# One relative-table turn a step earlier, and two row sums a few turns earlier, in a relative-position attention stage

## The reference

```
logits = einsum('bhqd,bhkd->bhqk', q, k) + einsum('bhqd,qkd->bhqk', q, rk)
w = softmax(logits)
out = einsum('bhqk,bhkd->bhqd', w, v) + einsum('bhqk,qkd->bhqd', w, rv)
x = x + out @ Wo.T + bo
```

## Time and profile before

| what | value |
|---|---|
| median of three executions | 4339.19 us |
| profiled execution | 4342.39 us, span 4340.7 us |
| PE (matmul) busy over the span | 3962.5 us, 91% |
| DVE busy | 3486.0 us, 80% |
| ACT busy | 2981.4 us, 69% |
| POOL busy | 1446.1 us, 33% |
| mean granted TensorE clock | 0.951 |

### The profile page before, as it was taken

The page is one execution under the profiler, slowest core; times in us unless marked ns, Lnnn a source line. Parts: engine busy times, 40 slices in busy tenths (PEclk is TensorE's granted clock), DMA queues, the critical chain, the costliest instruction groups (busy, mean ns, idle before and its releaser), DMA issues. The chain is left out here.

```text
span 4340.7 us, 77253 instructions
## 1 busy us (share of the span) xinstructions
PE 3962.5 (91%) x26592; PEld 2108.1 (49%) x26592; DVE 3486.0 (80%) x6304; ACT 2981.4 (69%) x5821; POOL 1446.1 (33%) x1405
## 2 busy tenths in 40 slices
PE   8699999999999999996799999999999996599997
PEld 5355555555455555544433333333333333499997
DVE  6788888888888888835688898888888872477775
ACT  4078888888788878881148888888888883266664
POOL 0356666666666666641100000000000001522232
PEclk9599999999999999998879999999999997699998
DMA  8566666666676667635652323223323303676664
GB/s 312 152 160 171 165 171 165 170 165 170 159 172 165 170 160 172 164 81 188 201 99 31 53 38 47 44 40 46 50 36 48 43 7 89 172 218 172 170 179 110
DMA packets 486195, 556.39 MB, mean 128 GB/s; under 512 B 60260, under 2 KB 426836, under 8 KB 476524
## 3 DMA queue, kind: packets, MB, share of 16 engines
q1 hardware_dynamic: 465980, 526.94, 49.1%
q0 software_dynamic: 19824, 24.52, 3.4%
HBM read 347.67 MB, written 206.76 MB: 128 GB/s over the span
## 5 line engine op out<-in xcount | busy, mean ns | idle before, releaser
L371 DVE TENSOR_REDUCE pa_pm<-pa_psA 128x2 f32<-128x1024 f32 x1024 | 1207.9, 1219 | 134.9 <-PE pa_psA L460 134.8
L1098 ACT ACTIVATE ra_p<-ra_psS 128x512 f32<-128x512 f32 x2048 | 1082.0, 606 | 315.1 <-PE ra_psS L1175 223.8
L434 ACT ACTIVATE pa_p<-pa_psS 128x512 f32<-128x512 f32 x2048 | 1063.5, 604 | 247.4 <-PE pa_psS L486 243.1
L1009 DVE TENSOR_REDUCE ra_pm<-ra_psA 128x1 f32<-128x896 f32 x1024 | 1112.7, 1087 | 147.6 <-PE ra_psA L1133 132.7
L486 PE MATMUL pa_psS<-pa_qs,pa_zs 50*128 50x512 f32 x2048 | 793.2, 464 | 77.6 <-ACT pa_p L434 64.2
L460 PE MATMUL pa_psA<-pa_zs,pa_qs 48*128 48x512 f32 x2048 | 796.7, 472 | 38.0 <-DMA pa_zs<-k_halves 17.8
L1133 PE MATMUL ra_psA<-ra_zs,ra_qs 48*128 48x512 f32 x2048 | 729.9, 450 | 19.1 <-DVE ra_pm L1011 8.4
L1175 PE MATMUL ra_psS<-ra_qs,ra_zs 50*128 50x512 f32 (+3 forms) x2176 | 699.6, 406 | 28.4 <-ACT ra_p L1098 17.9
L486 PEld LDWEIGHTS pa_psS<-pa_qs,pa_zs 50*128 50x128 f32 x2048 | 342.2, 185 | 626.0 <-ACT pa_p L434 607.0
L1206 PE MATMUL ra_psO<-ra_p,ra_vs 128*32 128x512 f32 (+3 forms) x6400 | 551.0, 449 | 0.0
L1175 PEld LDWEIGHTS ra_psS<-ra_qs,ra_zs 50*128 50x128 f32 x2176 | 350.4, 186 | 409.0 <-ACT ra_p L1098 318.4
(11 more groups left out here) (247 smaller groups left out, 4947.2 us busy)
## 6 DMA issues: line engine op xcount, KB each, us to landing
relative_rows<-ra_rst SPq DMA_DIRECT2D x128, 512.0 KB, 3.9
ra_blk<-window_rows SPq DMA_DIRECT2D x128, 512.0 KB
mo_w_raw<-ffn_W SPq DMA_DIRECT2D x58, 1024.0 KB, 5.4
ra_zs<-k_halves SPq DMA_DIRECT2D x192, 248.0 KB, 7.1
ra_dl<-relative_rows SPq DMA_DIRECT2D x128, 256.0 KB, 4.7
window_rows<-ra_pc SPq DMA_DIRECT2D x128, 256.0 KB
pa_qs<-q_halves SPq DMA_DIRECT2D x192, 128.0 KB, 6.2
pa_zs<-k_halves SPq DMA_DIRECT2D x192, 128.0 KB, 6.8
```

Source lines behind the costliest of these rows:

```text
L371: dve.reduce_max(pm[:, par, 2 * a:2 * a + 2], psA[w][:, :, :], AX.X).then_inc(s_am.h, 1)
L434: act.activation(pr[:, i % NPR, :], psS[:, slot(i), :], ACT.Exp).then_inc(s_ex.h, 1)
L1009: dve.reduce_max(pm[:, q, i, 2 * left:2 * left + 1], psA[w][:, lo:lo + 2 * G - P], AX.X).then_inc(s_far.h, 1)
L1098: act.activation(dst, psS[:, slot(i), :], ACT.Exp if kind == "E" else ACT.Copy).then_inc(s_cp.h, 1)
```

## The change

Two tuples of numbers change. The fourth `R` turn (piece c = 3) moves from step 5 to step 4, and sums 0 and 1 move from behind turns 13 and 18 to behind turns 10 and 17. In `SUM_TURNS` the numbers count turns of the new body, in which turn 13 is the `R` and the score turns that were T13 and T14 are T14 and T15.

```diff
-R_STEPS = (1, 2, 3, 5)
+R_STEPS = (1, 2, 3, 4)
...
-SUM_TURNS = (13, 18, 23, 28)
+SUM_TURNS = (10, 17, 23, 28)
```

## The result

The changed kernel took 4419.7 us (median of 4 runs, 4396.9 to 4430.7) beside 4340.8 for the kernel before on the same chip. All 30 runs of it on record lie between 4381.0 and 4430.7 us, with a median of 4407.0; the ratio on record, 1.0151 [1.0121 to 1.0181], answers to these (4407.0 / 4340.8 = 1.0152) and not to the median of four. The forecast of 4360.5 had the sign and a quarter to a third of the size, and the time is far outside the range of 4346 to 4372. The profiled execution took 4403.5 us against 4342.4, which is +61.1; its stage of relative scores, from the first O0 to the 31st (30 heads), went from 1639.3 to 1697.5 us, +58.2. So the loss lies where it was looked for.

What follows compares the result with a forecast made beforehand. PE was taken to bound the relative stage, with DVE close behind. 30 x 0.83 = 24.9 us lost, less 3.6 given back, is +21.3; against the median 4339.2 that makes 4360.5 us, range 4346 to 4372.

Steps and rivals of the forecast that it cites:

- Its chain: Steps 3 to 5 of a head: delayed buffer releases make PE wait, so each head takes 0.83 us longer.
- Sum 1 at nothing: Moving sum 1 one score turn earlier was counted as nothing; at best it would give back 0.60 us a head.
- only R3's wait: Rival, 13%: in step 4 DVE hides sum 0, leaving 0.38 us a head; 4348.7 us.
- Absorbed later: Rival, 10%: a later PE makes its 13.9 us of waits for ACT go; +7.4 us, 4346.6 us.
- Faster: Rival, 8%: R3 slides into slack in step 4 and a later score turn gains; -0.79 us a head, 4315.5 us.
- sums dearer: Rival, 5%: DVE takes up the next instruction only well after a sum; 1.32 us a head, 4375 us.
- the first step: Reading the relative stage's profile: PE busy 392.20 of 400 us, granted clock 1.00, so PE sets the pace.
- the term that was summed: The longer head in the relative stage: 30 heads at 0.83 us each, 24.9 us.
- The prediction's own test: Wrong if O4 to O5 is 3.7 us or less, a later step shortens by as much, or other steps move.
- The give-back of 3.6 us: PE's waits for GpSimd's folds, 4.2 us in five heads, were to shrink by 3.6 us as PE runs 0.83 later.
- an R turn was said to cost its 0.75 and a wait: In step 3, R2 costs PE 0.75 us plus a wait if too little precedes the turn after next.

Runs made afterwards that it cites:

- the two parts: Two runs against the kernel before: only R3 moved to step 4, ratio 1.0013; only sum 0 moved behind the copy of R2, ratio 1.0020.

## Why the prediction was wrong

Its chain held, step by step. R3's start 1.13 behind O4, the waits of 0.46 and 0.41 (measured 0.47 and 0.34), O4 to O5 and O5 to O6 are as worked out, and so is the head, +0.82 for +0.83. Sum 1 at nothing: shown by its run alone. The rival "only R3's wait" is refuted by the two parts, 0.39 and 0.34 a head. "Absorbed later" is refuted: PE's wait for ACT is 15.0 us, not less than the 13.9 of the earlier trace rows. "Faster" and "sums dearer" are refuted by the rows: T13 waits 0.47, and the turn behind the sum starts 0.59 behind it. By the rule that the prediction took from the Trainium skill ("VectorE: DVE Perf Modes", The DRAIN you can't avoid) it would have been 1.09; the prediction left out that the same section says of a next operation that is not held back that it starts earlier, and the 0.59 agrees with that.

**What failed is the first step**, the reading of the earlier trace rows: "the granted clock is 1.00". It was taken as a property of the stage and not as a state that the change could end, and no term and no rival stood on it. The cost of a fall was so put at nothing, without a reason. It is worth +28.3 us in the profiled execution, about half of its +61.1, while the term that was summed, 24.9, came out at 24.6. The timed runs bear it out: their mean clock over the whole execution is 0.933 to 0.947 in the 30 of the kernel after and 0.949 to 0.955 in those of the kernel before. The 30 scatter over 50 us, and 25 of the kernel before on one chip over 19, as one expects of a cost that comes in some heads and not in others. The prediction's own test caught it: "I am wrong ... if other steps of the head move at all", and steps 6 and 7 do, in the heads with a long fall. The rule that I left out is in the Trainium skill, "TensorE: Matmul & The Clock Gate", A second HAM failure mode: psum-queue depth-cycling. It tells, of another kernel in bf16, of short idle times between groups of matmuls, as banks of PSUM are cycled, that make the clock go down and up. That is the kind of wait which this change adds, and the trace agrees as far as that the fall follows waits of 0.48 and 0.35 us; what of PE's work counts, no run here settles.

**The give-back of 3.6 us was wrong too.** It rested on the folds being set by GpSimd and R0 and R1 alone, with PE 0.83 later. PE's wait for the folds in fact grew, from 4.2 us in 5 places to 7.5 in 6, one of them of 2.3. In all eight other kernels with R3 in step 4 it did shrink, to between none and 3.1 us; the two with the DVE order of the kernel after and repeated fills have 2.8 and none. So the direction was right for these, by up to 4.2 us. Why it grew in the kernel after stays open: the falls don't explain it, since R3 issued twice has 13 of them and 0.8 us of this wait, and there is one profile of each kernel.

**A part of the reasoning that did not matter**: an R turn was said to cost its 0.75 and a wait. In step 3 it costs 0.46, since five fills want 3.26 us there anyway.

## What to carry to other kernels

Price a wait that you add to a loop bound by TensorE twice: its length, and what a fall of the clock behind it would cost. A mean clock of 1.00 says nothing of how near it is to a fall, and 0.4 us a head decided here between a loss of 0.2% and one of 1.5%. Try a change that moves two things in its parts and together: two moves that were harmless apart were not so together. And look for the heads that don't look like the others before you explain the mean.

## What was not expected of the hardware

- A fall of the clock can begin about 1 us behind waits of 0.3 to 0.5 us each, though PE is busy in 1575 of 1640 us (96%). A fall of 3.4 us cost 1.5 us, one of 6.8 us 3.0, and one of 13.7 us 5.5.
- Matmuls that fill the waits do not simply prevent it: 11 falls became 4 at one dose of waits, and 26 stayed 26 at a larger one.
- Three falls in one profile came with longer waits (1.27 us for GpSimd, then 10.2 us at half clock; 1.65 us for GpSimd, then 3.4; and 13.7 us that began during a wait of 2.96 for DVE), in a kernel whose median is no different from before.
